# A loop body on TensorE that begins at another of its steps

## What is computed

```python
x = x + sin(einsum('oc,chw->ohw', W, coord) + b)        # per channel, the same for both images
x = x + bias[None, :, None, None]
x = upfirdn(x, 2 * up_filter, up=2)                     # 12 taps, rows and columns: 512 x 512
x = leaky_relu(x, 0.2) * sqrt(2)
x = upfirdn(x, down_filter, down=2)                     # 12 taps, rows and columns: 256 x 256
```

## Time and profile before

| | |
|---|---|
| median of 3 runs | 6414.84 us (6413.83 to 6424.86) |
| the profiled execution | 6412.11 us |
| its span, first to last instruction | 6410.3 us |
| TensorE matmul busy | 6212.8 us, 97% |
| TensorE weight load busy | 6125.1 us, 96% |
| VectorE busy | 3766.7 us, 59% |
| ScalarE busy | 4340.8 us, 68% |
| GpSimd busy | 1313.1 us, 20% |
| mean granted TensorE clock | 0.998 of full speed |
| DMA | 85 GB/s, 27.3% of 16 engines |

### The profile page before, as it was taken

How to read it: one execution, slowest core, us unless ns; L and a number is a source line. 1 busy time by engine, 2 the same in 40 slices (tenths; PEclk the granted TensorE clock), 3 DMA queues, 4 the chain that set the end, 5 groups by cost and what they waited for, 6 DMA issues and landing times.

```text
span 6410.3 us, 673809 instructions
## 1 busy us (share of the span) xinstructions
PE 6212.8 (97%) x299008; PEld 6125.1 (96%) x299008; DVE 3766.7 (59%) x6208; ACT 4340.8 (68%) x9224; POOL 1313.1 (20%) x1038
## 2 busy tenths in 40 slices
PE   5999999999999999999999999999999999999998
PEld 5999999999999999999999999999999999999998
DVE  5555555555555555555555555555555555555554
ACT  4666666666666666666666666666666666666666
POOL 1222222222222222222222222222222222222221
PEclk9999999999999999999999999999999999999999
DMA  2222222222222222222222222222222222222222
GB/s 71 86 86 86 86 86 86 86 86 86 86 86 86 86 86 86 86 86 86 86 86 86 86 86 86 86 86 86 86 86 86 86 86 86 86 86 86 86 86 72
DMA packets 568426, 546.87 MB, mean 85 GB/s; under 512 B 37968, under 2 KB 565328, under 8 KB 568400
## 3 DMA queue, kind: packets, MB, share of 16 engines
q1 hardware_dynamic: 568400, 546.47, 27.3%
HBM read 274.75 MB, written 271.58 MB: 85 GB/s over the span
## 4 chain that ended last, share of the span: by engine, by line
PE 97%; issue 2%; DVE 1%; ACT 0%; DMA 0%; SPq 0%; POOL 0%; DVEq 0%; ACTq 0%; POOLq 0%
PE a_ps L435 34%; PE p_ps L435 29%; PE y_ps L435 29%; PE y_ps L451 5%; DVE up_band L363 0%; DVE angle L342 0%; DVE angle L344 0%; DVE phase L334 0%; ACT trig L253 0%; DVE turns L338 0%; DVE turns L340 0%; DVE angle L346 0%; DVE down_band L365 0%; DMA bias_cols<-in_L_conv_bias_dram 0%; POOL x_sum L240 0%
## 5 line engine op out<-in xcount | busy, mean ns | idle before, releaser
L384 DVE SCALAR_TENSOR_TENSOR z<-y_ps,leak 128x512 f32<-128x512 f32 x4096 | 2638.5, 685 | 1341.7 <-ACT leak L266 1341.6
L435 PE MATMUL y_ps<-up_band,a_sb 64*64 64x138 f32 (+2 forms) x65536 | 3016.9, 278 | 5.1 <-issue 4.7
L266 ACT ACTIVATE leak<-y_ps 128x512 f32<-128x512 f32 x4096 | 2240.8, 604 | 211.5 <-PE y_ps L435 211.4
L435 PE MATMUL p_ps<-down_band,z 64*64 64x40 f32 (+1 forms) x131072 | 2356.9, 223 | 11.3 <-issue 9.5
L435 PEld LDWEIGHTS p_ps<-down_band,z 64*64 64x64 f32 x131072 | 2336.4, 135 | 10.2 <-issue 10.1
L240 POOL TENSOR_TENSOR x_sum<-x_raw,f_sb 128x512 f32<-128x512 f32 x1024 | 1306.5, 1276 | 5049.5 <-DVE f_sb L392 4424.4
L435 PEld LDWEIGHTS y_ps<-up_band,a_sb 64*64 64x64 f32 x65536 | 2280.9, 133 | 41.5 <-issue 7.4
L435 PE MATMUL a_ps<-up_band,x_sum 64*64 64x138 f32 (+2 forms) x32768 | 1571.7, 281 | 149.2 <-issue 121.3
L435 PE MATMUL a_ps<-down_band,p_rows 64*64 64x40 f32 (+1 forms) x65536 | 1479.7, 223 | 2.7 <-ACT p_rows L280 1.2
L272 ACT COPY o_out<-a_ps 128x256 f32<-128x256 f32 x2048 | 662.4, 375 | 1196.8 <-PE a_ps L435 1196.8
L435 PEld LDWEIGHTS a_ps<-down_band,p_rows 64*64 64x64 f32 x65536 | 1367.2, 135 | 5.8 <-issue 5.8
(11 more groups left out here) (26 smaller groups left out, 39.4 us busy)
## 6 DMA issues: line engine op xcount, KB each, us to landing
x_raw<-in_x_dram SPq DMA_DIRECT2D x1024, 256.0 KB, 2.7
out_dram<-o_out SPq DMA_DIRECT2D x1024, 256.0 KB, 2.2
f_rows<-trig_dram SPq DMA_DIRECT2D x1024, 6.0 KB
trig_dram<-trig SPq DMA_DIRECT2D x8, 256.0 KB, 2.4
trig_dram<-ones SPq DMA_DIRECT2D x4, 128.0 KB, 1.8
trig_dram<-bias_wide SPq DMA_DIRECT2D x4, 128.0 KB, 1.7
up_taps<-in_L_conv_up_filter_dram SPq DMA_DIRECT2D x1, 6.0 KB, 2.3
down_taps<-_L_conv_down_filter_dram SPq DMA_DIRECT2D x1, 6.0 KB, 2.4
```

Of the source, the lines that this page charges most:

```text
L266: nc.scalar.mul(leak[i % 2][:, :], y_ps[i][:, :], SLOPE * GAIN).then_inc(leak_done, 1)
L384: nc.vector.scalar_tensor_tensor(z[n][:, i, :], y_ps[i][:, :], GAIN, leak[i % 2][:, :], ALU.mult, ALU.max).then_inc(z_done, 1)
L435: last = nc.tensor.matmul(outs[o][half * HALF:(half + 1) * HALF, lo:hi], data[row, where[k], col:col + HALF], band[row, start:start + hi - ...
```

## The change

`slot` is cut in two: `ups`, the four up steps, and `downs`, all that follows. The sequence of steps stays as it was. The loop, which went over ups(c, 0), downs(c, 0), ups(c, 1), downs(c, 1), now goes over downs(c, 0), ups(c, 1), downs(c, 1), ups(c + 1, 0). ups(2, 0) therefore stands ahead of the loop, and what follows it begins with downs(C - 2, 0). No other engine's program is changed.

```diff
-            def slot(c, n, a_next=True, f_next=True, y=True, p=True, o=True, f_before=True, first=False):
+            def ups(c, n, a_next=True, y=True, f_before=True, first=False):
                 m = 2 * c + n
                 if a_next:
                     up_rows(m + 1, 1 - n, 0, first)
...
                     up_rows(m + 1, 1 - n, 1)
                 if y:
                     up_cols(m, n, 0, 1)
+
+            def downs(c, n, a_next=True, f_next=True, y=True, p=True, o=True):
+                m = 2 * c + n
                 if p:
                     down_rows(m - 1, 1 - n, 0)
...
-            slot(0, 0, p=False, o=False, first=True)
-            slot(0, 1, o=False, first=True)
-            slot(1, 0, first=True)
-            slot(1, 1)
+            ups(0, 0, first=True)
+            downs(0, 0, p=False, o=False)
...
+            ups(1, 1)
+            downs(1, 1)
+            ups(2, 0)
 
             with pe.Fori(2, C - 2) as c:
-                slot(c, 0)
-                slot(c, 1)
-            slot(C - 2, 0)
-            slot(C - 2, 1, f_next=False)
...
+                downs(c, 0)
+                ups(c, 1)
+                downs(c, 1)
+                ups(c + 1, 0)
+            downs(C - 2, 0)
+            ups(C - 2, 1)
+            downs(C - 2, 1, f_next=False)
...
```

More of the change, by code:

```diff
@@ L544, in _ @@
             sines(1, 0)
-            slot(0, 0, p=False, o=False, first=True)
-            slot(0, 1, o=False, first=True)
-            slot(1, 0, first=True)
-            slot(1, 1)
-            with pe.Fori(2, C - 2) as c:
-                slot(c, 0)
-                slot(c, 1)
-            slot(C - 2, 0)
-            slot(C - 2, 1, f_next=False)
[L555 to L558, removed]
+            ups(0, 0, first=True)
+            downs(0, 0, p=False, o=False)
+            ups(0, 1, first=True)
+            downs(0, 1, o=False)
+            ups(1, 0, first=True)
+            downs(1, 0)
+            ups(1, 1)
+            downs(1, 1)
+            ups(2, 0)
+            with pe.Fori(2, C - 2) as c:
+                downs(c, 0)
[5 more added lines that the diff above has]
+            downs(C - 2, 1, f_next=False)
+            ups(C - 1, 0, f_before=False)
+            downs(C - 1, 0, f_next=False)
+            ups(C - 1, 1, a_next=False)
+            downs(C - 1, 1, a_next=False, f_next=False)
+            downs(C, 0, a_next=False, f_next=False, y=False)
+            downs(C, 1, a_next=False, f_next=False, y=False, p=False)
 _INS = ["x", "L0_conv_W", "L0_conv_b", "L1_conv_bias", "L1_conv_up_filter", "L1_conv_down_filter"]
```

## The result

| | before | after |
|---|---|---|
| median of 4 runs each | 6419.12 us (6413.83 to 6424.86) | 6264.92 us (6262.96 to 6267.45) |
| span of the profiled execution | 6410.3 us | 6261.2 us |
| period of two images (the turn) | 12.33 us | 12.03 us |

The changed kernel takes 0.9756 of the time (95% interval 0.9744 to 0.9769): 154 us less, 0.30 us for each of the 507 turns taken. The forecast was 6329 us, 0.17 us a turn.

The account below looks back on a forecast made before the run. It took TensorE unfed at the loop's turn as the bound: 0.62 us removed less 0.45 added (0.39 hole, 0.06 halting) gains 0.17 per turn, 86 us over 507 turns, from 6414.84 to 6329 us; range 6265 to 6400.

Parts of the forecast that it names:

- What bounds the kernel: TensorE unfed at the loop's turn, once per 12.33 us; no semaphore of another engine ends its waits there.
- Removal, 0.62 us: Old turn between p_ps and a_ps steps: its whole cost, 0.62 us per turn, goes.
- (a): New turn, increment to first p_ps load: 0.76 us, with two register and two semaphore instructions behind the branch.
- rival 1: Shorter chain: one register instruction suffices or a semaphore instruction goes; 0.11 less, gain 0.28 a turn, 6273 us; chance 0.14.
- (b): New turn: y_ps loads still starting behind the increment hide 0.3 us of the sequencer's work, against 0.19 at the old place.
- rival 3: Full cover: sequencer over 0.76 us ahead in the up steps, no hole left, gain 0.62 a turn, 6101 us; chance 0.03.
- (c): New turn, last y_ps to first p_ps load: hole of 0.46 us, 0.07 there anyway, so 0.39 lost.
- (d): p_ps loads behind the new turn's branch come haltingly: 0.06 us added per turn, bounds 0 and 0.13.
- straight code costs the same on either side: Four up steps written out ahead of the loop instead of behind it: taken as 0, plus or minus 5 us.
- The sum: New turn costs 0.45 us against 0.62 removed: 0.17 us gained per turn, 86 us over 507 turns.
- (2): The turn costs the same at both places: gain 0 to 0.03 us a turn, 6400 to 6415 us; chance 0.07.
- (4): Slower: the taken branch waits until the array has started what is queued; 0.07 us a turn worse, 6451 us; chance 0.09.

Follow-up runs that it names:

- b_plus12: Kernel before with 12 idle semaphore instructions ahead of the loop, so its head lies one past a block's bound: 6321.52 us, ratio 0.9846.
- e_holes: Kernel before with five idle instructions ahead of the second image's first a_ps step, four ahead of the first image's first p_ps step: 6939.81 us.
- e_slot60: Kernel before with its loop's head placed at instruction 60 of a block of 256, by one jump ahead of the loop: 6323.23 us, ratio 0.9851.

## Why the prediction was right and wrong

**What bounds the kernel**: right. The time was TensorE unfed at the turn, and no wait of another engine took over, in any run.

**Removal, 0.62 us**: sized about right, put together wrongly. The old hole gave 0.36 (1438 to 1077 ns; 0.09 of a hole stays, where the second p_ps step leads to a0 with three sequencer instructions between them), and the halting up steps with what follows them 0.185, together 0.55. The prediction noted the halting (0.08 "and more"), and had it inside the 0.62, so the sum took it as gained; what it missed is why it was there. That the size came near is luck: a third of the 0.55 went because the loop's head moved in the code, not because the turn moved in the work.

**(a) Chain, 0.76**: 0.69 in the mean. One register instruction, not two; the two semaphore instructions start 0.11 us apart in two thirds of the turns and 0.16 in the others (0.72 in the turn shown). That is rival 1's condition (the numbers fit into one instruction), worth 0.07 here instead of its 0.11.

**(b) Cover, 0.3**: right, 0.31. The 64 entries that the prediction quoted from the Trainium skill ("TensorE: Matmul & The Clock Gate", Architectural detail, Engine queue depths) were not reached at any of the four places: the cover was 0.19 to 0.41 us, where the prediction's estimate from the page was 0.90. Full cover (rival 3) did not come, although the best place came near it.

**(c) Hole, 0.39 lost**: 0.325 against b_plus12, the kernel with the old turn and a harmless head (y01 from 457 to 782 ns). Oversized by 0.065, nearly all of it from the chain.

**(d) Halting loads, +0.06, bounds 0 and 0.13**: this is the step that failed. It took the halting as something a jump does to the loads behind it, which would move along with the turn and hurt p_ps more than a_ps. It belonged to the head's place in the code. At the harmless place that the changed kernel has, the p_ps step is 0.06 *faster* than with no turn (989 to 928 ns in b_plus12 and after), as behind the made holes of e_holes; at the bad place it takes 1148, 0.22 more than at the harmless one and 0.16 more than with no turn. Neither was inside the bounds. The sentence "straight code costs the same on either side" failed in the same way: four up steps (132 instructions) written out ahead of the loop moved its head from 1976 to 2108, off the bad place, and that is worth 94 to 101 us of a gain of 154.

**The sum**: added 0.325, less 0.06 in the p_ps step and 0.02 in smaller steps, 0.25 instead of 0.45; removed 0.55 instead of 0.62. 0.55 - 0.25 = 0.30 a turn. Of the 0.13 by which that exceeds the forecast, (d) made 0.12 and the hole 0.065; the removal took 0.07 back. Had the head stayed at the bad place, the gain would have been about 51 us, which the forecast's 86 overstates, and the time about 6368.

**The rivals**: (1) came closest in time, 6273, and its condition held, but that was worth 0.07 us a turn, about half of the difference; its time was met by luck. (2) and (3) didn't occur. (4) fell: COMPARE_BRANCH lasted 207 or 208 ns at the new place in nearly all turns, as at the old one, while loads went on starting for 0.1 to 0.3 us after it began, so its length did not follow what was queued.

## What to carry to other kernels

A loop's turn costs its engine the chain of sequencer instructions from the increment to the first instruction behind the jump, less the work still queued at that point. Choose the place where few waits and register operations follow and where much is queued ahead; each instruction behind the jump was worth 0.12 us a turn, and the price of the turn went from 0.36 us at the old place to 0.25 at the new and 0.01 at the best of the four. Before any change that moves code is credited with its gain, look at where the loop's head falls: a control with a few idle instructions ahead of the old loop costs one run, and told here that some three fifths of the gain did not come from the turn's new place.

## What the runs showed of the hardware that was not expected

- TensorE's code came in blocks of 256 instructions. A loop head eleven instructions short of a block's bound cost 0.185 to 0.20 us at each jump (94 to 101 us over 507), in halting loads behind it. With the head 20 short, one past, 135 short and 196 short no loads halted (the old loop took 6334 us at 20 short, 6322 at one past and 6323 at 196 short). Nothing was tried between 11 and 20, or nearer than 11.
- A body of 1211 instructions stayed on the core for 507 turns (23 packets on the instruction queue in all); one of 2419 was fetched anew in each of 254 turns, at 23 us a turn and 1.87 times the time. Where between them it tips was not tried.
- In the loops whose body stays, a taken COMPARE_BRANCH on TensorE took 207 to 216 ns at all four places in the work, with or without a hint, and one not taken 76 to 83. It took 4040 ns in the median where the body did not stay, and 1.83 us once, on the jump that the placing of e_slot60's head adds. The Trainium skill ("Advanced Engine Details and Errata", Control Flow Timing) gives about 108 ns for a compare-and-branch; neither 208 nor 76 agrees.
- The first p_ps step took 0.93 us behind a hole of 0.26 to 0.61 us, 0.06 less than the 0.99 of the same step without one (b_plus12), so a hole costs a little less than its length.
